# Linear attention with a mixture-of-experts gate, one core: reciprocals of the denominators spread by DMA instead of by matmuls

## The reference

```python
qp, kp = phi(LN(x) @ Wq.T + bq), phi(LN(x) @ Wk.T + bk)      # phi = elu + 1
v = LN(x) @ Wv.T + bv
# per token t of a sequence, per head:
kv   = kv + outer(k_t, v_t)
ksum = ksum + k_t
num  = q_t @ kv
den  = dot(q_t, ksum) + 1e-6
o_t  = num / den
x = x + (o @ Wo.T + bo)
x = x + moe(LN(x))        # top 2 of 8 experts; experts over capacity are dropped whole
```

## Time and profile before

| | |
|---|---|
| median of three runs | 1914.15 us (1913.77 to 1918.07) |
| profiled execution, its own time | 1916.06 us |
| its span | 1914.3 us |
| granted TensorE clock | 0.998 |
| PE busy | 1890.7 us, 99% |
| DVE busy | 1569.2 us, 82% |
| POOL busy | 889.8 us, 46% |
| ACT busy | 663.8 us, 35% |
| DMA | 217.97 MB, 114 GB/s |

### The profile page before, as it was taken

How to read it: one execution, slowest core, us unless ns; L and a number is a source line. 1 busy time by engine, 2 the same in 40 slices (tenths; PEclk the granted TensorE clock), 3 DMA queues, 4 the chain that set the end, 5 groups by cost and what they waited for, 6 DMA issues and landing times.

```text
span 1914.3 us, 60181 instructions
## 1 busy us (share of the span) xinstructions
PE 1890.7 (99%) x25412; PEld 1659.6 (87%) x25412; DVE 1569.2 (82%) x3356; ACT 663.8 (35%) x1298; POOL 889.8 (46%) x981
## 2 busy tenths in 40 slices
PE   7999999999999999999999999999999999999997
PEld 6888888888888888888888888888888888888887
DVE  7888787888879888778878888887888897888888
ACT  4333333323333332333333433333333333323331
POOL 4345554455443554534554445544345553455422
PEclk9999999999999999999999999999999999999999
DMA  6343234333243432343323334333443234333222
GB/s 215 101 128 112 96 106 128 118 118 112 90 127 119 127 121 74 123 125 116 123 89 118 117 112 136 100 98 113 128 128 112 85 114 130 117 117 113 89 73 90
DMA packets 171197, 217.97 MB, mean 114 GB/s; under 512 B 24368, under 2 KB 85808, under 8 KB 170928
## 3 DMA queue, kind: packets, MB, share of 16 engines
q1 hardware_dynamic: 170928, 214.13, 35.4%
HBM read 151.02 MB, written 63.04 MB: 112 GB/s over the span
## 4 chain that ended last, share of the span: by engine, by line
PE 95%; DVE 2%; POOL 1%; DMA 1%; issue 0%; SPq 0%; ACT 0%; POOLq 0%; DVEq 0%
PE ring L684 38%; PE ring L666 36%; PE ring L758 7%; PE num_ps L788 6%; PE num_ps L771 3%; PE num_ps L801 2%; PE ring L730 1%; PE ring L743 1%; DMA v_tok<-in_wv_t 1%; DVE s_mask L973 0%; PE ring L654 0%; DVE stats L1091 0%; DVE den L1220 0%; DVE res L1084 0%; DVE o_lo L1215 0%
## 5 line engine op out<-in xcount | busy, mean ns | idle before, releaser
L1315 POOL TENSOR_TENSOR k_sum<-k_sum,q_raw 128x512 f32<-128x512 f32 x128 | 165.3, 1291 | 545.0 <-DVE q_raw L984 545.0
L883 ACT ACTIVATE e_tmp<-ring,bias_n 128x512 f32<-128x512 f32 x256 | 175.9, 687 | 509.3 <-PE ring L666 508.7
L973 DVE TENSOR_TENSOR s_mask<-ring,causal 128x512 f32<-128x512 f32 x512 | 315.0, 677 | 0.0
L684 PE MATMUL ring<-wv_hi,xt_hi 128*128 128x260 f32 x1024 | 298.9, 292 | 0.0
L684 PE MATMUL ring<-wv_hi,xt_lo 128*128 128x260 f32 x1024 | 289.2, 282 | 0.0
L684 PE MATMUL ring<-wv_lo,xt_hi 128*128 128x260 f32 x1024 | 289.2, 282 | 0.0
L684 PE MATMUL ring<-wo_hi,o_hi 128*128 128x260 f32 x1016 | 284.8, 281 | 1.3 <-ACT o_hi L938 1.3
L684 PE MATMUL ring<-wo_lo,o_hi 128*128 128x260 f32 x1016 | 285.7, 282 | 0.0
L684 PE MATMUL ring<-wo_hi,o_lo 128*128 128x260 f32 x1016 | 285.5, 284 | 0.2 <-DVE o_lo L1215 0.2
L938 ACT ACTIVATE o_hi<-num_ps 128x512 fp32r<-128x512 f32 x127 | 75.8, 597 | 465.9 <-PE num_ps L788 465.9
L666 PE MATMUL ring<-xt_hi,wk_hi 128*128 128x512 f32 x512 | 207.2, 405 | 3.4 <-DVE xt_lo L1042 1.7
(11 more groups left out here) (147 smaller groups left out, 3955.4 us busy)
## 6 DMA issues: line engine op xcount, KB each, us to landing
x_tok<-in_x SPq DMA_DIRECT2D x128, 256.0 KB, 3.8
res<-in_x SPq DMA_DIRECT2D x128, 256.0 KB, 2.8
out<-res SPq DMA_DIRECT2D x128, 256.0 KB, 2.1
x_in<-in_x_t SPq DMA_DIRECT2D x124, 256.0 KB, 4.7
keys_turned<-k_turned SPq DMA_DIRECT2D x112, 256.0 KB, 2.0
k_tok<-keys_turned SPq DMA_DIRECT2D x448, 64.0 KB, 2.1
x_rows<-moments_rows SPq DMA_DIRECT2D x31, 512.0 KB, 3.6
k_t<-in_wk_t SPq DMA_DIRECT2D x4, 256.0 KB, 4.5
```

Of the source, the lines that this page charges most:

```text
L684: mm = pe.matmul(bank[:, 0:HW], rows[a](k), w[b][:, k, h, :], start=n == 0, stop=n == 3 * KD - 1)
L883: act.activation(e_tmp[:, m], bank, ACT.Relu, bias=bias_n[:, m, g:g + 1], scale=-1.0).then_inc(phi_relu.handle, 1)
L973: dve.tensor_tensor(s_mask[:, j], ring[:, st.bank(u)].rearrange("p (g t) -> p g t", g=KD), repeat(causal, KD), ALU.mult).then_inc(free[st. ...
L1315: pool.tensor_tensor(k_sum[:, g], k_sum[:, g], q_raw[:, g], ALU.mult).then_inc(prod.handle, 1)
```

## The change

The reciprocals take another way to the rows of the queries. PE sums the denominators with one place per token tile, so that `den` is 128x128 (rows: tile, then head) and not 128x256. ACT evicts it ahead of the numerators, and DVE takes the reciprocal ahead of the numerators' low parts. SP then sends the two halves of `den` to DRAM (two tiles of tokens each) and fetches each back with every head's row repeated over its 32 rows, 128 rows of 4 KB, into the memory of `k_sum`. DVE divides in two operations, each over all queries' features for 256 tokens, one at the start of tile 3 and one behind the values of tile 2. The rounding on ACT, the two-part operation on DVE, the spreading matmuls, their four uses of the ring and the constants for them go. The denominators' matmuls stand in front of `from_tile`. The steps that choose experts get their own scratch `choice`. The moments of tile 2's residual are taken ahead of the division instead of behind it.

```diff
-SKIPS = {0: 1, 3: 2}
+SKIPS = {3: 1}
...
-        uses += [("O", (c, 0)), ("O", (c, 1))] + [("R", g) for g in range(KD)] * (c == 2)
+        uses += [("O", (c, 0)), ("O", (c, 1))]
...
+    rden = k_sum.rearrange("p g t -> p (g t)").rearrange("p (h g t) -> p h g t", h=2, g=KD)
...
-    scratch = (den, rden_high.bitcast(F32))
+    scratch = (choice[:, 0], choice[:, 1])
...
+        def send_reciprocals(b):
+            sp.wait_ge(den_rec.handle, b + 1)
+            for half in range(2):
+                rows = den[half * P // 2:(half + 1) * P // 2]
+                sp.dma_start(den_dram[half].rearrange("r s t -> s r t"), rows).then_inc(den_out[half].handle, 16)
+
+        def spread_reciprocals(b):
+            for half in range(2):
+                sp.wait_ge(den_out[half].handle, 16 * (b + 1))
+                rows = den_dram[half, 0:HPG * KD].rearrange("(j g) s t -> j (g s t)", g=KD).unsqueeze(1)
+                sp.dma_start(rden[:, half].rearrange("p g t -> p (g t)"), rows.to_broadcast([HPG, HD, D * 2])
+                             ).then_inc(den_in[half].handle, 16)
...
                 if c == 2:
                     send_keys(t, 3)
+                    if st.has("proj"):
+                        send_reciprocals(t + 1)
+                        spread_reciprocals(t + 1)
                     fetch_keys(t, 3)
...
             for g in range(KD):
-                for s in range(2):
-                    mm = pe.matmul(bank[g * HD:(g + 1) * HD, 0:BT // 2], head_cols[:, s],
-                                   k_sum[:, g, s * BT // 2:(s + 1) * BT // 2], start=s == 0, stop=s == 1,
-                                   tile_position=(0, g * HD))
+                for s in range(TPB):
+                    mm = pe.matmul(bank[s * HD:(s + 1) * HD, 0:P], head_cols[:, g],
+                                   k_sum[:, g, s * P:(s + 1) * P], start=g == 0, stop=g == KD - 1,
+                                   skip_group_check=True, tile_position=(0, s * HD))
             mm.then_inc(full[st.bank(u)].handle, 1)
-
-        def spread_reciprocals(st):
...
+            if c % 2 == 0:
+                pe.wait_ge(divided.handle, 2 * off + c // 2 + 1)
...
                     from_state(st, c)
                     add_state(st, c)
+                    if c == 2 and proj:
+                        denominators(st)
                     from_tile(st, c)
...
+                if c == 2 and proj:
+                    u = ("DEN", 0)
+                    act.wait_ge(full[st.bank(u)].handle, st.filled(u))
+                    act.activation(den, ring[:, st.bank(u), 0:P], ACT.Copy, bias=DEN_EPS
+                                   ).then_inc(free[st.bank(u)].handle, 1)
...
+        def invert(st):
+
+            dve.wait_ge(free[BANK[("DEN", 0)]].handle, st.freed(("DEN", 0)))
+            dve.reciprocal(den, den).then_inc(den_rec.handle, 1)
+
+        def divide(st, half):
+
+            dve.wait_ge(den_in[half].handle, 16 * (st.off + 2))
+            t = slice(half * BT // 2, (half + 1) * BT // 2)
+            dve.tensor_tensor(q_div[:, (st.off + 1) % 2, :, t], rden[:, half], q_raw[:, :, t], ALU.mult
+                              ).then_inc(divided.handle, 1)
...
                 if last and proj and attn:
-                    divide(st)
-                if last and attn and proj:
-                    residual_moments(st, 2)
+                    divide(st, 0)
                 if proj:
                     chunks(st, c, 0, 1)
-                if last and not attn:
-                    divide(st)
+                if last and proj and attn:
+                    divide(st, 1)
...
                 if attn:
                     residual(st, c)
-                    if c != 2 or not proj:
-                        residual_moments(st, c)
+                    residual_moments(st, c)
```

More of the change, by code:

```diff
@@ L349, in set_biases @@
         dve.tensor_tensor(gw_bo, gw, over(bo_col, E), ALU.mult).then_inc(bias_set.handle, 1)
[L351 to L361, removed]
     def set_gates(dve):
@@ L416, in set_constants @@
         link(pool.memset(head_cols, 0.0))
-        for s in range(2):
-            for h in range(2):
-                row = 2 * HPG * s + HPG * h
-                link(pool.tensor_copy(head_cols[:, s, row:row + HPG], head_of_row))
+        for g in range(KD):
+            rows = head_cols[:, g, 0:HPG * KD].rearrange("p (j g) -> p j g", j=HPG)
+            link(pool.tensor_copy(rows[:, :, g], head_of_row))
         link(pool.memset(kv_diag, 0.0))
-        link(pool.memset(row_of_group, 0.0))
-        for g in range(KD):
-            link(pool.affine_select(out=row_of_group, in_=row_of_group, compare_op=ALU.not_equal, fill=1.0,
-                                    base=-g * HD, pattern=[[-1, 2 * 2 * HPG]], channel_multiplier=1))
         for e in range(E):
@@ L1024, in turn_keys @@
                           ).then_inc(keys_turned.handle, 1)
-        def divide(st):
-            for g in range(KD):
-                u = ("R", g)
-                dve.wait_ge(full[st.bank(u)].handle, st.filled(u))
-                bank = ring[:, st.bank(u)]
-                dve.tensor_tensor(q_div[:, (st.off + 1) % 2, g], bank, q_raw[:, g], ALU.mult).then_inc(free[st.bank(u)].handle, 1)
+        def invert(st):
[6 more added lines that the diff above has]
+                              ).then_inc(divided.handle, 1)
         def normalise_first(c):
@@ L1201, in body @@
                     split_x_low(st, 1)
+                if last and not attn:
+                    divide(st, 0)
                 if c == 2 and attn:
@@ L1207, in body @@
                     turn_keys(st.off, 2)
+                if c == 2 and proj:
+                    invert(st)
                 if st.alone() and last:
@@ L1217, in body @@
                     sum_state(st, c)
-                if c == 2 and proj:
-                    dve.wait_ge(free[BANK[("DEN", 0)]].handle, st.freed(("DEN", 0)))
-                    dve.reciprocal(den, den).then_inc(den_rec.handle, 1)
                 if not last and attn:
@@ L1228, in body @@
                     chunks(st, c, 2, 3)
-                if c == 2 and proj:
-                    dve.wait_ge(rden_hi.handle, rden_hi.at(st.lin(1, st.off + 1, 1)))
-                    dve.scalar_tensor_tensor(rden, rden_high.bitcast(F32), lo_rows, den,
-                                             ALU.mult, ALU.add).then_inc(rden_parts.handle, 1)
                 if c < 2 and attn and turns:
```

50 lines of the change are left out of this document (12 added, 38 removed).

## The result

The changed kernel takes 2169.62 us, the median of four runs (2167.16 to 2178.15), against 1914.38 for the kernel before, measured beside it. The ratio is 1.134, with a 95% interval of 1.130 to 1.137: 255 us slower. The prediction was 1940 in a range up to 1960. The profiled execution took 2178.15 us for a span of 2176.4, which is 262.1 more than before.

The account below looks back on a forecast made before the run. The prediction took PE, busy for 1890.7 of 1914.3 us, to bound the kernel. From 1914.15 it subtracted 14.1 and 4.8 us of PE work and added 45 us of waits: 1940 us, range 1904 to 1960.

Parts of the forecast that it names:

- What bounds the kernel: Whole kernel: PE, busy 1890.7 of 1914.3 us; a microsecond less on PE is one less of time unless PE waits.
- PE's part, 18.9 us: PE, 32 steps: removed spreading matmuls save 0.44 us each (14.1 us), denominators' new shape 0.15 each (4.8 us).
- The round trip: Reciprocals by SP's DMA to DRAM and back: both halves arrive before their divisions, so the transfers cost nothing.
- The keys' fetch: Tile 3's keys, queued behind the spreads: land at 929.5, or 931 at worst, before first use at 931.14 less 0.44.
- The divisions, 45 us: VectorE after tile 2's output: divisions meet POOL at the SBUF port; PE waits 1.5 us at 30 block boundaries.
- the mark: Time in a block where PE has finished the attention output of tile 2; 927.03 us in the predicted block.
- The transfers are late: Rival: divisions wait for reciprocals' DMA, 1.5 us and more; PE waits 2 to 3 us a block; 1955 to 1985, chance 0.1.
- the main case: Divisions collide with POOL and PE waits at block boundaries: 1940 us, within 1922 to 1960, chance 0.62.
- What would show it: Profile signs: spreading matmuls gone, denominators 0.9 us a step, divisions 2.0 to 2.6 us, first projection waiting 1 to 2 us.

Follow-up runs that it names:

- x2: Changed kernel with each half spread by four DMAs of 32 rows, each source one row repeated 32 times; 1959.0 us, ratio 1.0216.
- x7: x2 with POOL's normalising of tile 3 and its bias on tile 3's residual cut to a few columns; 1919.95 us, ratio 1.0017.
- x16: x14 with SP's load of the next block's first residual moved behind the keys' sending and fetch; 1916.6 us, ratio 1.0006.
- x14: x2 with the second division behind tile 3's residual (first step: masks), keys' fetch between halves, tile 2's moments behind tile 3's residual; 2027.3 us, ratio 1.0594.
- x11: Kernel before with its four divisions' reciprocal operand read from a constant SBUF tile instead of PSUM; 10073 us in total, as the experts' program runs.

## Why the prediction was wrong

**What bounds the kernel:** right. PE's stalls came out in the time, though one that stands ahead of another in the same block, as the keys' in x2, is not added to it.

**PE's part, 18.9 us:** nearly right in the sum, wrong in its parts. Removing the spreading matmuls saves 0.66 us a step, not 0.44: from the start of tile 2's output to the end of the values behind it PE took 6.49 us before and takes 5.83 now. The output in front of them (2.97 instead of 2.87) and the values behind them (3.08 instead of 2.96) were slower next to them. The denominators save nothing. I compared 1.03 with 0.88, but the longer one is whichever stands in front of the scores: before, numerators 0.88 and denominators 1.03; after, denominators 0.88 (1042.43 to 1043.31) and numerators 1.02 (to 1044.33). Together about 21 us.

**The round trip: the step that failed.** "A spread of the same shape as each new one (128 rows of 4 KB) lands in 3.6" took the duration of `x_rows<-moments_rows`. The shape in SBUF and the bytes are the same, but that transfer repeats one source row 128 times, and the new ones repeat four rows 32 times each. The source's first dimension is 4, and 4 engines work. I had the first half in at 925.5 and the second some 2 us later; 5.1 us of transfer each, one behind the other, put the divisions 9.3 and 14.4 us behind the issue. "I cost the transfers at nothing" should have been 211 us (after against x2). The rest of the chain held well enough: the halved reciprocal takes 0.95 us, and the small write lands within 2.5, where 1.4 was forecast and 3.8 at worst.

**The keys' fetch:** "929.5, or 931 at worst", "covered, closely at worst". By its own figures the worst case is not covered: 931 against 931.14 less 0.44. It was 8.2 us late in the block shown, 7.9 in the mean of 16, the largest single wait, since it queues behind both spreads. With the wide form it is late by 0.9 us in the mean and 2.0 at most (x7).

**The clock:** no step had it. In the block shown PE's matmuls behind the stall ran at a granted clock of 0.52, and over the run its busy time grew by about 73 us more than its work explains.

**The divisions, 45 us:** right in mechanism and nearly in size, but hidden in the changed kernel, where data come so late that POOL is mostly done: 54 of the 64 divisions take 1.22 or 1.23 us. With the transfers mended, x2 shows divisions of 2.56 and 1.49 us, the last low part of x 13.4 us behind the mark (13.31 forecast) and a projection 13.5 behind it (13.41 forecast). That PE would be there after 11.94 was off, and the nearness of 13.5 to 13.41 hides it: before took 12.38 and 12.08 us in turn, of which the spreads' removal takes 0.56, so that PE would be there after 11.82 and 11.52. PE loses 1.84 us a block, not 1.47, and 55 us in all. x7 takes 39 of them back; the late keys, which cost nothing beside the collision, come out there. The place of PE's wait was too simple too: it is split between a wait in tile 3, for the keys or for the masks, and one before the projection.

**The rivals:** "The transfers are late" had the right mechanism, with a chance of 0.1 and a price of 1955 to 1985. It allowed 5 us for a spread, which is what one took, but then had the second 2 us behind, as if both shared 16 engines, and no price for the keys. x2 at 1959 is where the main case would have ended, inside the range of 1904 to 1960 but 19 us above the 1940. Less the 2.5 us by which before was slower on that chip that is 1956.5. The forecast has the stall 10 us too small, lacks the later start (5.8) and the slower projections behind the waits (27 times 0.14, 4 us), and has PE's gain 2 too small, which makes 1958 against these 1956.5.

**What would show it:** "If PE waits for scores or for the keys' fetch instead, the transfers were the cause" is what the profile showed.

## What to carry to other kernels

Before a transfer is taken as costing what another of the same size costs, compare the first dimension of its source and of its destination as the instruction carries them: a DMA share that stands at 0.25 or 0.13 while it is alone in flight means that 4 or 2 engines do the work. Here cutting it so that a dimension of 32 came first repaired it, and cutting it so that one of 2 came first made it worse. When an operand of VectorE moves from PSUM to SBUF, look at what GpSimd does at that time: here the divisions met it and lasted up to 2.66 us instead of 1.22. Moving work off a bound engine is worth only what the waits behind it leave: taking 0.66 us a block off PE gained 0.15 (x16), because VectorE's last low part was then what PE waited for. Such a wait can be missing from the list of waits; compare the end of what is waited for with the start of what waits. When an operation is moved, follow each semaphore that it signals to the queues that wait on it: one load in front of the keys cost 110 us (x14 against x16).

## What the runs showed of the hardware

- 512 KB from DRAM into 128 rows took 5.1 us at 102 GB/s with the source's first dimension 4, and 10.0 us at 51 GB/s with 2; with 128 it landed in 4.3 us beside other traffic, and as four transfers of 32 rows in 2.9 each.
- The granted clock was 1.00 from 1059 to 1060 us and 0.50 from 1060 to 1061, with PE idle since 1054.9. It was 0.52 in the 4 us after the stall (1063 to 1067), with PE busy for 3.91 of them; the next 4 us had 1.00.
- Groups of short matmuls took longer or shorter by their neighbours: the same 32 records took 0.88 us, or 1.02 in front of the scores, and the eight spreading matmuls cost 0.66 us where their own stretch is 0.44.
- PE's first projection took 5.67 us instead of 5.53 where it had waited for VectorE, if only 0.1 us (x7).
- DVE and POOL held each other in both directions. A division of 1.22 us took 2.56, and POOL's addition of 1.33 took 2.28 in the same meeting (x2). The Trainium skill, "SBUF — State Buffer", "Who interferes with whom", says that an instruction of VectorE with two inputs in SBUF contends with one of GpSimd that reads SBUF, over a shared pair of ports. x7, with POOL's work cut (1205 ns a division), and x11, with nothing but the operand moved to SBUF (1489 ns a division, and 5.85 us for four instead of 2.49), agree.
